# A graph layer on one core: the halves of a mixing pass redrawn on four engines

## The reference, cut to what matters

```python
xn = layernorm(x)                                   # x: 6250 nodes x 256
g  = relu(segment_sum(h[src] * norm, dst) + b)      # 200000 edges, h = xn @ W
# _L0_mix_ref(xn[None], ...): 8 heads of 32, one batch of 6250 rows
q, k, v = split(xn @ Wqkv.T);  q, k = elu(q) + 1, elu(k) + 1
kv = einsum('nshd,nshm->nhmd', k, v);  ksum = k.sum(axis=1)
z  = 1 / (einsum('nlhd,nhd->nlh', q, ksum) + 1e-6)
t  = einsum('nlhd,nhmd,nlh->nlhm', q, kv, z)
x1 = layer_norm(t + xn, ln1_g, ln1_b)
h  = gelu(x1 @ W1.T + b1)
m  = layer_norm(h @ W2.T + b2 + x1, ln2_g, ln2_b)
x  = x + g + m
x  = x + ffn(layernorm(x))       # 8 experts, top 1, capacity 977
```

## Time and profile before

| | us |
|---|---|
| median of 3 runs (2458.11 to 2458.78) | 2458.72 |
| the profiled execution, its own time | 2454.8 |
| its span, from the first to the last instruction | 2453.0 |
| PE busy | 2157.4 (88%) |
| DVE busy | 1770.2 (72%) |
| ACT busy | 1213.4 (49%) |
| POOL busy | 366.4 (15%) |
| first and last attention product (L1231) | 515.5 and 1520.3 |
| first and last second-norm sum (L1891) | 559.2 and 1558.4 |

### The profile page before, as it was taken

How to read it: one execution, slowest core, us unless ns; L and a number is a source line. 1 busy time by engine, 2 the same in 40 slices (tenths; PEclk the granted TensorE clock), 3 DMA queues, 4 the chain that set the end, 5 groups by cost and what they waited for, 6 DMA issues and landing times. The chain is left out here.

```text
span 2453.0 us, 41210 instructions
## 1 busy us (share of the span) xinstructions
PE 2157.4 (88%) x13789; PEld 1545.6 (63%) x13789; DVE 1770.2 (72%) x5676; ACT 1213.4 (49%) x2731; POOL 366.4 (15%) x396
## 2 busy tenths in 40 slices
PE   3739999998998999888899899999989995999997
PEld 2625655566666666666666666666656654999897
DVE  3564544478887888888888888866766754887886
ACT  0435544455555555555555555444444444655563
POOL 7100000001111111111111011100000002333432
PEclk7869999999999999999999999999999997999999
DMA  5000000000000000000000000000010004222220
GB/s 182 13 7 3 3 3 3 3 3 5 3 3 3 5 3 3 3 5 3 3 3 3 3 5 3 6 29 29 31 38 29 29 27 124 79 68 87 88 81 9
DMA packets 52135, 63.54 MB, mean 26 GB/s; under 512 B 15695, under 2 KB 44330, under 8 KB 51808
## 3 DMA queue, kind: packets, MB, share of 16 engines
q1 hardware_dynamic: 27104, 29.06, 3.7%
q0 software_dynamic: 10336, 21.41, 3.2%
q10 hardware_dynamic: 14496, 10.53, 1.3%
HBM read 42.82 MB, written 20.92 MB: 26 GB/s over the span
## 5 line engine op out<-in xcount | busy, mean ns | idle before, releaser
L1189 PE MATMUL p_m<-node_halves,adj 128*128 128x512 f16 x3626 | 986.5, 389 | 17.1 <-DVE rows_v L1813 14.2
L1574 ACT CAST adj<-p_b 128x392 f16<-128x392 f32 x1184 | 570.0, 485 | 843.0 <-PE p_b L1179 827.7
L1786 DVE TENSOR_TENSOR one_src<-iota,codes 128x512 bf16<-128x512 bf16 x1184 | 503.8, 425 | 428.7 <-PE p_b L1179 418.8
L1179 PE MATMUL p_b<-one_edge,one_src 128*128 128x98 bf16 x4736 | 613.3, 266 | 54.8 <-ACT adj L1574 39.6
L1179 PEld LDWEIGHTS p_b<-one_edge,one_src 128*128 128x128 bf16 x4736 | 458.3, 116 | 298.9 <-DVE one_src L1786 61.9
L1189 PEld LDWEIGHTS p_m<-node_halves,adj 128*128 128x128 f16 x3626 | 360.1, 105 | 246.5 <-issue 41.4
L1786 DVE TENSOR_TENSOR one_edge<-iota,codes 128x392 bf16<-128x392 bf16 x1184 | 429.0, 362 | 0.0
L1103 POOL TENSOR_TENSOR x1r<-x1n,bc_ln1g 128x256 f32<-128x256 f32 x49 | 44.9, 916 | 840.1 <-ACT x1n L1498 840.1
L1092 POOL DMA_INDIRECT src_e<-in_srcR,item_chunk x37 | 38.2, 1033 | 727.8 <-DVEq L1808 726.3
L1156 POOL DMA_INDIRECT out_dram<-oo,slot_node x64 | 74.8, 1168 | 219.7 <-DVE oo L2210 203.1
L1138 POOL DMA_INDIRECT rows<-node_features,slot_row x64 | 73.2, 1144 | 165.7 <-DVE slot_node L2317 146.6
(11 more groups left out here) (343 smaller groups left out, 3530.9 us busy)
## 6 DMA issues: line engine op xcount, KB each, us to landing
w1raw<-in_w SPq DMA_DIRECT2D x8, 1024.0 KB, 5.3
w2raw<-in_w SPq DMA_DIRECT2D x8, 1024.0 KB
res<-in_x SPq DMA_DIRECT2D x7, 896.0 KB, 7.5
node_features<-res ACTq DMA_DIRECT2D x20, 256.0 KB
out_dram<-res ACTq DMA_DIRECT2D x20, 256.0 KB
out_dram<-res SPq DMA_DIRECT2D x1, 1152.0 KB
fb_b<-in_fb SPq DMA_DIRECT2D x1, 1024.0 KB, 9.2
rows<-node_features,slot_row POOLq DMA_INDIRECT x64, 4.9
```

The costliest lines, as they stand in the source:

```text
L1179: mm = pe.matmul(p_b[n % 2][:, u * HI2:(u + 1) * HI2], one_src[:, n % ONER, :, u], one_edge[:, n % ONER, :, u], start=True, stop=True)
L1189: mm = pe.matmul(p_m[:], adj[:, k % 2, h, :], node16[:, h, :], start=(h == 0), stop=(h == NBLK - 1))
L1574: nc.scalar.copy(adj[:, n // SPV % 2, :, n % SPV * 2 * IB:(n % SPV + 1) * 2 * IB] .rearrange("p h (u r) -> p h u r", r=2), p_b[n % 2][:, 0 ...
L1786: V.tensor_tensor(tile[:, n % ONER], iota4[:, 0:m, :], codes[:, q % 2, a, at:at + IB].rearrange("p (m u) -> p m u", m=1) .broadcast_to([P, ...
```

## The change

Attention moves from half 11 of its pass to half 0 of the next; turning of the first norm's rows from half 9 to half 2 of the pass after; the hidden products from half 4 to 5 and into the free half of the bank `p_y`; the output products from 9 to 10. On ScalarE Gelu and exponential move from 5 and 7 to 6 and 8, `normalised_y` from 6 to 7, `normalised_t` from 8 to 10, `x1T` from 10 to 3 of the next pass, `x_normalised` from 11 to 9. VectorE's `finish` moves from 7, 8, 9 to 9, 10, 11; GpSimd's two operations from 9 and 10 to 11 and 0. `transposes_x1` no longer waits for the Gelu but, as block `b+2` is turned before it, for `xnT` of that block; `hidden` waits for the Gelu and the second norm's sum of the block before, and no longer for `xnT`.

```diff
-        X_AT, Q_AT, Y_AT, A_AT = 0, 4, 9, 11
+        X_AT, A_AT, T_AT, Q_AT, H_AT, Y_AT = 0, 0, 2, 4, 5, 10
...
         def attended(b):
-            return steps_by(first_mix + b, A_AT)
+            return steps_by(first_mix + b + 1, A_AT)
 
         def x1_turned(b):
-            return steps_by(first_mix + b + 1, Y_AT)
+            return steps_by(first_mix + b + 2, T_AT)
 
         def hidden_made(b):
-            return steps_by(first_mix + b + 2, Q_AT)
+            return steps_by(first_mix + b + 2, H_AT)
...
-                    if k == 9 and 0 <= c < NBLK:
+                    if k == 11 and 0 <= c < NBLK:
                         row_scaled(c)
-                    if k == 10 and 0 <= c < NBLK:
-                        row_biased(c)
+                    if k == 0 and 0 <= c - 1 < NBLK:
+                        row_biased(c - 1)
...
             def transposes_x(b):
                 t_.wait_ge(xn_ok, b + 1)
-                wait(t_, x1T_ok, (b - 1) * CH)
+                wait(t_, x1T_ok, (b - 2) * CH)
...
             def transposes_x1(b):
                 t_.wait_ge(x1n_ok, b + 1)
-                t_.wait_ge(xnT_ok, min(b + 2, NBLK))
-                wait(t_, gelu_ok, b * CH)
+                t_.wait_ge(xnT_ok, min(b + 3, NBLK))
...
             def hidden(b):
                 t_.wait_ge(x1T_ok, b * CH + CH)
-                t_.wait_ge(xnT_ok, min(b + 3, NBLK))
+                wait(t_, gelu_ok, b * CH)
+                wait(t_, y_sum, b)
                 for m in range(CH):
                     for a in range(CH):
-                        pe.matmul(p_t[:, m, :], w1t_sb[:, a, m * P:(m + 1) * P], x1T[:, a, :],
+                        pe.matmul(p_y[:, C + m * P:C + m * P + P], w1t_sb[:, a, m * P:(m + 1) * P], x1T[:, a, :],
                                        start=(a == 0), stop=(a == CH - 1))
...
-                if k == Q_AT:
-                    if 0 <= b - 2 < NBLK:
-                        hidden(b - 2)
-                    if b < NBLK:
-                        queries(b)
-                if k == Y_AT:
-                    if 0 <= b - 2 < NBLK:
-                        output(b - 2)
-                    if 0 <= b - 1 < NBLK:
-                        transposes_x1(b - 1)
-                if k == A_AT and b < NBLK:
-                    attention(b)
+                if k == A_AT and 0 <= b - 1 < NBLK:
+                    attention(b - 1)
+                if k == T_AT and 0 <= b - 2 < NBLK:
+                    transposes_x1(b - 2)
+                if k == Q_AT and b < NBLK:
+                    queries(b)
+                if k == H_AT and 0 <= b - 2 < NBLK:
+                    hidden(b - 2)
+                if k == Y_AT and 0 <= b - 2 < NBLK:
+                    output(b - 2)
...
-                    nc.scalar.activation(gT[:, a, :], p_t[:, a, :], ACT.Gelu, bias=g["cols"]["b1"][:, a:a + 1]
+                    nc.scalar.activation(gT[:, a, :], p_y[:, C + a * P:C + a * P + P], ACT.Gelu, bias=g["cols"]["b1"][:, a:a + 1]
...
-                if k == 5 + 2 * (b % 2) and 0 <= b - 2 < NBLK:
+                if k == 3 and 0 <= b - 2 < NBLK:
+                    x1_transposed(b - 2)
+                if k == 6 + 2 * (b % 2) and 0 <= b - 2 < NBLK:
                     gelu(b - 2)
-                if k == 7 - 2 * (b % 2) and b < NBLK:
+                if k == 8 - 2 * (b % 2) and b < NBLK:
                     queries(b)
-                if k == 6 and 0 <= b - 3 < NBLK:
+                if k == 7 and 0 <= b - 3 < NBLK:
                     normalised_y(b - 3)
-                if k == 8 and 0 <= b - 1 < NBLK:
+                if k == 9 and b + 1 < NBLK:
+                    x_normalised(b + 1)
+                if k == 10 and 0 <= b - 1 < NBLK:
                     normalised_t(b - 1)
-                if k == 10 and 0 <= b - 1 < NBLK:
-                    x1_transposed(b - 1)
-                if k == 11 and b + 1 < NBLK:
-                    x_normalised(b + 1)
...
-                    for n, at in enumerate((7, 8, 9)):
+                    for n, at in enumerate((9, 10, 11)):
                         if k == at:
                             finish(b - 3, n)
```

## The result

| | before | changed |
|---|---|---|
| median, us | 2458.41 (2456.60 to 2458.78) | 2377.41 (2372.76 to 2380.05) |
| profiled execution, its own time / span | 2454.8 / 2453.0 | 2380.05 / 2378.3 |
| stretch of the passes in the trace | 1060.0 | 984.4 |

Each kernel has four runs. The ratio is 0.9666, 95% interval 0.9655 to 0.9678: 81 us faster, where 47 were forecast. The time lies 7 us under the range, nearest to the rival in which nearly all comes off (2384).

The account below looks back on a forecast made before the run. TensorE was taken to bound the stretch, with VectorE nearly level. Gains of -64 and +17 given back make -47: 2454.8 less 47 is 2408, plus 3.9 for the median is 2412 us, range 2384 to 2454.

Parts of the forecast that it names:

- the rival in which nearly all comes off: Passes over node blocks: removed waits, build waits and clock come off almost whole, -75 us to 2384; chance 14%.
- attention wait: TensorE's attention products waiting for VectorE's queries, 27.8 us; one half more of distance takes off 24 us.
- turning: `x1n` gone, `xnT` new: TensorE's transposes of the first norm's rows: 17.6 us wait goes, about 6 us for ScalarE's `xnT` copy comes; -12.
- output product on the Gelu: TensorE's output product waiting 17.7 us for ScalarE's Gelu; 6 kept, so -12 us, through ScalarE's shorter wait for the roots.
- builds on the copies: TensorE's adjacency builds waiting 16.3 us for ScalarE's copies; 8 kept, so -8 us.
- given back by VectorE: VectorE, nearly level with TensorE, makes it wait for one-hots and `rows_v`; a quarter of the gain returns, +17 us.
- clock: TensorE's granted clock, now and then at 0.50, costs 11 to 16 us in the stretch; half returns, -8 us.
- The new wait for `xnT`: TensorE's transposes at half 2 wait for ScalarE's copy at half 1: 6 x 0.9 + 12 x 0.07 = 6 us.
- ScalarE's run of halves 8 to 10: ScalarE's load, queries, norm rows and copies, 4.6 to 4.7 us in three halves; costed at 0, up to 30 without cover.
- `kf` never waits for `ke`: Sign against the forecast: VectorE's queries operation `kf` waiting for ScalarE's `ke` would show it wrong.
- ScalarE's wait for the roots: ScalarE's `normalised_y` waiting for VectorE's roots, 55.5 us in 45 waits; three quarters go, about 15 left.
- The sums of 931 against 959 us: Stretch of the passes: VectorE without its build waits 931 us, TensorE without its waits 959, so nearly level.

Follow-up runs that it names:

- The load runs: 156 extra VectorE operations of 0.42 us added to the kernel before (ratio 1.0103), to it with only attention moved (0.9931), and to the changed kernel (0.9740).
- turning alone: Changed kernel with attention back at half 11, `normalised_y` at 6, `finish` at 7, 8, 9; turning, hidden, output and ScalarE's other moves stay: ratio 0.9822.
- attention and second norm: Kernel before with attention at half 0 of the next pass, `normalised_y` at half 7 and `finish` at 9, 10, 11: 2413.7 us, ratio 0.9818.
- the second norm alone: Kernel before with only `normalised_y` at half 7 instead of 6 and `finish` at 9, 10, 11 instead of 7, 8, 9: 2455.9 us, ratio 0.9969.

## Why the prediction was right in sign and too small in size

| step | predicted | measured in the stretch |
|---|---|---|
| attention wait | -24 | -24.2 |
| turning: `x1n` gone, `xnT` new | -12 | -17.6 + 2.9 |
| output product on the Gelu | -12 | -12.3 |
| builds on the copies | -8 | -9.3 |
| given back by VectorE | +17 | +4.2 (`rows_v`) + 1.9 (one-hots) |
| clock | -8 | -10.2 |
| shorter busy time, clock aside | not in the sum | -8.2 |
| sum | -47 | -75.6 (with 3 us of small waits) |

**What held.** Where TensorE lost its time, and how much each named wait would lose: the first four lines, -56 predicted, are within 5 us. The new wait for `xnT` was placed rightly and priced too high: 6 us, from six bad passes of 0.9 and twelve others of 0.07 (why twelve, of the 43 left, the text doesn't say), against 2.9 in four waits. The hidden products' bank costs nothing, as said (0.9680 against 0.9666, 983.6 against 984.4 us of stretch). ScalarE's run of halves 8 to 10 did no harm (the builds' wait for copies fell from 16.3 to 7.0), and `kf` never waits for `ke`. ScalarE's wait for the roots came out at 8.1 where about 15 was named. The Trainium skill's drain of 1.38 us behind a table load ("ScalarE: Activation LUTs", "What ACT_TABLE_LOAD costs") is not in the trace after either; ScalarE's load and the Gelu behind it stand 1.30 us apart:

```profile
991.59 1.28 ACT L1509 ACT_TABLE_LOAD   x1
...
992.89 0.63 ACT L1509 ACTIVATE gT<-p_y,col_b 128x128 f32<-128x128 f32 x2
```

**What failed first: "I take a quarter of the gain back, +17".** It came back as 6, which is 11 of the 28.6 us by which the stretch was missed. (A quarter of 64 is 16; the sum has 17.) VectorE did lose its waiting, and more of it than was forecast: 55.4 us are left where 70 to 85 were named, and still only 6 came back. The step counted VectorE's lag twice. It was already in the 27.8 us of the attention wait, because the queries, one half ahead of their user, were the narrowest place between the two engines; the one-hots have two steps of ring. The load runs bear this out: the same extra work adds 17.1 us of idle time with attention at half 11 and 2.9 with attention at half 0 (27 and 13 us of stretch, the difference being half clock). In the changed kernel it adds 11.6, so there the room is not free; that its give-back is only 6 is measured, and that it has this reason is inferred from the other two. The sums of 931 against 959 us said that the engines were level in the mean; they said nothing on where a lag would be felt.

**What failed second: busy time and small waits were put at nothing.** I gave the clock 8 and nothing to anything else. From 1060.0 to 984.4 the idle time explains 57.2. The half clock went from 30.7 us to 10.2, half of the difference is 10.2. The remaining 8.2 is TensorE's busy time for the same matmuls. About 4 of it are the attention products themselves, of which 30 of 49 groups stood behind a wait before and 8 do after (TensorE's busy time at that line is the first number behind the comma):

```profile
500.00:1560.00 1060.00, 35.30 (x196) 26.16 (x196) 0.99 0.01 4
```

```profile
500.90:1485.30 984.40, 31.29 (x196) 25.70 (x196) 0.99 0.01 4
```

With attention alone moved it is 31.0, with attention alone put back 34.4. All in all 125 waits stand in the stretch before and 79 after, 0.18 us for each. Over the 17 traces TensorE's busy time follows 926.4 + 0.47 x half clock + 0.14 x number of waits within 1.6 us. That is an association, not a run that isolates it, and as the ends of matmuls are modelled in this profile, the border between busy and idle time is soft.

On top of the idle time nothing can be relied on. The stretch fell by 26.4 for 20.8 of idle time with attention alone, by 34.9 for 32.4 with turning alone, by 40.3 for 40.5 with attention and second norm, by 75.6 for 57.2 with all, and it rose by 2.5 for a fall of 9.0 with the second norm alone. The clock makes most of the difference.

**What was placed wrongly without hurting the sum.** I hung the Gelu's 12 us on ScalarE's wait for the roots. With that wait back (51.6 us) the Gelu's wait stays at 7.0: either edit removes it, `normalised_y` out of the roots' way, or, as the order of the halves suggests, a half of its own before the late Gelu. What the wait for the roots costs is builds, 14.1 + 18.7 against 7.0 + 7.7. By TensorE's idle time the three parts alone give 20.8, 9.0 and 32.4, 62.2 together, against 57.2 for all; by the ratios 1.2, 0.3 and 1.8%, 3.3 together, against 3.3. Even so they act on each other: in idle time the second norm's part is worth 9.0 alone and 19.7 behind attention, and turning 32.4 alone and 16.6 as the last part. GpSimd's scaling was said to run behind the queries now; it starts ahead of them in 23 of 49 passes (48 before), and 14 `finish` operations still take 0.7 us or more (17 before). It no longer matters, since TensorE asks for the queries later.

**The two references.** The forecast stood on the profiled execution, 2408, and added the 3.9 us by which the median of before lay above it. The profiled execution of the changed kernel is the slowest of its four, 2.6 above their median. So 28 of the 35 us by which the time was missed are the stretch, the rest is this.

**Left open.** How much half clock a kernel gets. With nearly equal idle time (60.1 us) the kernel with `normalised_y` at 6 has 10.2 us of it and the one with attention and second norm 37.5; two executions of the changed kernel have 10.2 and 17.1. Neither the number of waits (102 and 104 in the first two) nor of those above 1 us (13 and 14) orders them. So the 10 us of clock in the gain are measured in one pair of traces and not explained, and the second trace of the changed kernel would give 7.

## What to carry to other kernels

When an engine waits for another one at a fixed place in a written-out order, ask first which place has the least distance; a lag of the supplying engine is paid there, and it must not be charged again after the place is widened. Count a removed wait of the bound engine at its length; what came on top here lay between nothing and a third of the idle time, mostly with the clock, and can't be forecast from these runs. Of several moves that free each other, one that puts work ahead of a narrow place shows little of its worth alone (9 us of idle time here, 20 once that place was wide): try it again then. And compare parts by idle time beside the total: two equal totals can be made of different things.

## What the runs showed of the hardware

Two traces of the changed kernel from two chips differ by 50 us in the first 82 us of the program and by 4 in the stretch. The times of the kernel before differ in the same way: the kernel before took 2456.8 to 2462.4 us as a median in three sets of runs and 2408.7 to 2409.5 in two. Where it is slower, ScalarE and TensorE stand long at the start of the changed kernel (waits of its first 200 us), the one for something that the trace calls remote, the other for nothing that it shows; in the changed kernel's second trace, from a faster chip, these rows are missing and the stretch begins at 449.6 instead of 500.9.

```profile
ACT acc L624 <- remote: 53.8, 2, 47.1
...
PE p_tr L689 <- issue: 44.2, 1, 44.2
```

What they wait for is not settled by these runs.
